# GpSimd's neighbour gathers issued by half rounds, ahead of the maxima that use them

## What is computed

```python
cand = jnp.where(mask[..., None], h[:, None, :, :], NEG)   # mask: neighbours without the node itself
mx = cand.max(axis=2)
neigh_agg = jnp.where(has_neigh, mx, h)
out = h @ W_self + b_self + neigh_agg @ W_neigh + b_neigh
...
out = relu((out - mu) * rsqrt(var + EPS) * gamma + beta)
```

## Time and profile before

| | us |
|---|---|
| median of 3 runs | 9130.13 (9124.97 to 9143.81) |
| the profiled execution | 9111.52 |
| its span, first to last instruction | 9109.8 |
| busy: TensorE, VectorE, ScalarE, GpSimd | 5148.5, 5894.4, 4402.1, 5128.1 |
| granted TensorE clock, share of full speed | 0.781 |

### The profile page before, as it was taken

The page is one execution under the profiler, slowest core; times in us unless marked ns, Lnnn a source line. Parts: engine busy times, 40 slices in busy tenths (PEclk is TensorE's granted clock), DMA queues, the critical chain, the costliest instruction groups (busy, mean ns, idle before and its releaser), DMA issues.

```text
span 9109.8 us, 178961 instructions
## 1 busy us (share of the span) xinstructions
PE 5148.5 (57%) x60584; PEld 4779.8 (52%) x60584; DVE 5894.4 (65%) x7002; ACT 4402.1 (48%) x3608; POOL 5128.1 (56%) x5234
## 2 busy tenths in 40 slices
PE   3673750365765668365865667556845667362026
PEld 3672750364755557363865567555745567361025
DVE  5874860386867788486867687687847688581024
ACT  5644730165635566165735566356715566160034
POOL 0004777377764677377764677276764677377630
PEclk9885875687877878687987888788877888686568
DMA  2114332234332533135322433234322433132210
GB/s 99 43 34 124 66 66 25 46 69 113 61 63 65 122 65 80 19 76 133 67 62 66 119 66 83 58 75 101 69 48 66 120 65 80 54 55 58 23 26 29
DMA packets 307180, 629.05 MB, mean 69 GB/s; under 512 B 113553, under 2 KB 165906, under 8 KB 270610
## 3 DMA queue, kind: packets, MB, share of 16 engines
q0 software_dynamic: 91936, 161.87, 16.9%
q1 hardware_dynamic: 212354, 456.38, 14.2%
q10 hardware_dynamic: 2160, 0.06, 0.0%
HBM read 506.89 MB, written 111.15 MB: 68 GB/s over the span
## 4 chain that ended last, share of the span: by engine, by line
POOL 20%; issue 16%; DVE 14%; PE 13%; DMA 8%; ACT 4%; POOLq 2%; DVEq 2%; ACTq 1%; SPq 0%
DMA G<-table,idx 6%; POOL G L552 6%; POOL best L552 5%; PE ps L1413 4%; POOL best L538 4%; PE ps L1386 3%; PE ps L1415 2%; POOL best L535 2%; DVE keys L1077 2%; POOL G L535 2%; ACT Pbuf L689 1%; PE ps L1438 1%; DVE key L1067 1%; POOL best L537 1%; ACT Hn L689 1%
## 5 line engine op out<-in xcount | busy, mean ns | idle before, releaser
L552 POOL DMA_INDIRECT G<-table,idx x1416 | 1502.7, 1061 | 508.5 <-issue 452.7
L1415 PE MATMUL ps<-Hn,AT 128*128 128x99 bf16 x12288 | 1774.5, 216 | 0.0
L1415 PE MATMUL ps<-X,AT 128*128 128x99 bf16 x12288 | 1735.0, 214 | 52.6 <-issue 52.6
L544 POOL DMA_DIRECT2D idx<-lists x433 | 259.3, 599 | 2445.9 <-issue 1964.9
L689 ACT ACTIVATE Hn<-Rb,q 128x2048 int8<-128x2048 f32 x768 | 1485.4, 1988 | 86.6 <-PE ps L1415 82.1
L689 ACT ACTIVATE Pbuf<-Rb,q 128x2048 int8<-128x2048 f32 x768 | 1487.8, 1987 | 18.2 <-PE ps L1415 15.6
L552 POOL DMA_INDIRECT best<-table,idx x1024 | 1093.7, 1068 | 319.4 <-issue 309.3
L1415 PEld LDWEIGHTS ps<-X,AT 128*128 128x128 fp8e4 x12288 | 1243.2, 101 | 57.6 <-issue 57.6
L1415 PEld LDWEIGHTS ps<-Hn,AT 128*128 128x128 fp8e4 x12288 | 1256.5, 102 | 0.0
L1413 PE MATMUL ps<-X,Hn 128*128 128x198 bf16 x6144 | 933.6, 268 | 567.6 <-DVE Hn L937 358.6
L1413 PE MATMUL ps<-Hn 128*128 128x198 bf16 x6144 | 960.3, 272 | 433.0 <-DVE Zs L957 236.0
(11 more groups left out here) (186 smaller groups left out, 11171.7 us busy)
## 6 DMA issues: line engine op xcount, KB each, us to landing
Rb<-in_adj SPq DMA_DIRECT2D x128, 1024.0 KB, 6.3
Rb<-rrows SPq DMA_DIRECT2D x104, 1024.0 KB, 6.3
bytes_A<-A SPq DMA_DIRECT2D x128, 256.0 KB
bytes_AT<-AT SPq DMA_DIRECT2D x128, 256.0 KB
AT<-bytes_AT SPq DMA_DIRECT2D x128, 256.0 KB, 3.6
AT<-bytes_A SPq DMA_DIRECT2D x128, 256.0 KB, 4.6
G<-table,idx POOLq DMA_INDIRECT x1416
h<-Hn SPq DMA_DIRECT2D x16, 1024.0 KB, 4.1
```

The costliest lines, as they stand in the source:

```text
L544: pool.dma_start(idx[:, slot, :], lists[bass.ds(r, 1)].rearrange("o p k -> (o p) k")).then_inc(idx_in[slot], 16)
L552: pool.indirect_dma_start(out=dst[:, k, :], out_offset=None, in_=table, in_offset=bass.IndirectOffsetOnAxis(ap=idx[:, slot, k:k + 1], axis ...
L1415: ins = pe.matmul(both[:, 0, 0:G], A8[:, jb, at], v[:, 0:G], start=False, stop=jb == T - 1, skip_group_check=True)
```

## The change

`G` becomes the accumulator, with room for 4 keys, and `best` the place where gathers land, with two halves of 4. `idx` now holds two lists, `arrived_idx`, where the next list lands, and `asked`, from which the gathers in flight read; GpSimd copies one into the other by halves (128x4 elements). `ask(r, part)` makes this copy and issues 4 gathers. In a tile but the last, the first half of the first round is copied into `G`, and its place is asked for the next round at once; the second half is folded, and asked for again; then the list two rounds on is fetched. Further rounds do the same: wait for a half, fold it, ask for the same half of the next round, which may be that of the next tile. The last round of a tile asks for the first round of the next one. The last tile of a graph doesn't ask ahead: its first round is in flight already, and it asks for each further round at its start, both halves, and fetches the next list, which at the end is that of the next graph's first round. `gather` begins with asking for the first round. The fold of `best` onto itself loses its width 4, since `G` has 4 keys. Two more lists are reserved in HBM, and in the last `middle` SyncE writes one more list behind the last round, so that the last fetch finds one.

```diff
-        G = sb("G", [P, KEYS, F])
+        G = sb("G", [P, KEYS // 2, F])
         idx = sb("idx", [P, 2, KEYS], U32)
+        asked, arrived_idx = idx[:, 0, :], idx[:, 1, :]
...
-        LN_CHAIN, LV_CHAIN, POOL_CHAIN, MERGE, TREE = 7, 12, 4, 6, 10
+        LN_CHAIN, LV_CHAIN, POOL_CHAIN, MERGE, TREE = 7, 12, 4, 8, 7
...
             def middle(b, alone):
+                if alone:
+
+                    total = sp.value_load(cum[0:1, bass.ds(B * (T + 1) - 1, 1)], min_val=0, max_val=ROUNDS)
+                    plain(sp)
+                    sp.wait_ge(idx_ready, total)
+                    sp.wait_ge(list_in, total * 16 + 16)
+                    settle(sp)
+                    sp.dma_start(lists[bass.ds(total, 1)].rearrange("o p k -> (o p) k"), found_idx[:, :]).then_inc(list_in, 16)
...
-            def fetch(r, slot):
+            def fetch(r):
 
                 plain(pool)
                 pool.wait_ge(list_in, r * 16 + 32)
-                pool.dma_start(idx[:, slot, :], lists[bass.ds(r, 1)].rearrange("o p k -> (o p) k")).then_inc(idx_in[slot], 16)
-
-            def rows_of(fetched, slot, dst):
+                pool.dma_start(arrived_idx, lists[bass.ds(r, 1)].rearrange("o p k -> (o p) k")).then_inc(idx_in, 16)
+
+            def half(part):
+                return slice(part * (KEYS // 2), (part + 1) * (KEYS // 2))
+
+            def ask(v, r, part):
 
                 plain(pool)
-                pool.wait_ge(idx_in[slot], fetched * 16)
+                pool.wait_ge(idx_in, r * 16 + 16)
                 settle(pool)
-                for k in range(KEYS):
+                v(pool.tensor_copy(asked[:, half(part)], arrived_idx[:, half(part)]))
+                settle(pool)
+                for k in range(part * (KEYS // 2), (part + 1) * (KEYS // 2)):
                     pool.indirect_dma_start(
-                        out=dst[:, k, :], out_offset=None, in_=table,
-                        in_offset=bass.IndirectOffsetOnAxis(ap=idx[:, slot, k:k + 1], axis=0)).then_inc(got[k], 16)
+                        out=best[:, k, :], out_offset=None, in_=table,
+                        in_offset=bass.IndirectOffsetOnAxis(ap=asked[:, k:k + 1], axis=0)).then_inc(got[part], 16)
+
+            def landed(r, part):
+                plain(pool)
+                pool.wait_ge(got[part], r * 64 + 64)
 
             def number(b, t):
                 return pool.value_load(cum[0:1, bass.ds(b * (T + 1) + t, 1)], min_val=0, max_val=ROUNDS)
 
             def tile(b, t, last):
                 lo, hi = number(b, t), number(b, t + 1)
-
-
-
-
-                fetch(lo if last else lo + 1, 1)
-                rows_of(b * T + t + 1, 0, best)
-                if last:
-
-                    plain(pool)
-                    pool.wait_ge(idx_in[1], lo * 16 + 16)
-                pool.sem_inc(merged, MERGE)
+                v = Chain(pool, merged, lo * MERGE, MERGE)
+                landed(lo, 0)
+                settle(pool)
+                v(pool.tensor_copy(G[:, :, :], best[:, half(0), :]))
+                if not last:
+                    ask(v, lo + 1, 0)
+                landed(lo, 1)
+                greater(v, G[:, :, :], best[:, half(1), :])
+                if not last:
+                    ask(v, lo + 1, 1)
+                    fetch(lo + 2)
+                settle(pool)
+                pool.sem_inc(merged, MERGE - v.n)
                 with pool.Fori(lo + 1, hi) as r:
+                    w = Chain(pool, merged, r * MERGE, MERGE)
                     if last:
-                        fetch(r, 1)
-                    rows_of(r + 1 if last else r, 1, G)
-                    v = Chain(pool, merged, r * MERGE, MERGE)
-                    for half in range(2):
-
-                        plain(pool)
-                        for k in range(half * KEYS // 2, (half + 1) * KEYS // 2):
-                            pool.wait_ge(got[k], r * 16 + 16)
-                        if half == 1 and not last:
-
-                            fetch(r + 1, 1)
-                        part = slice(half * KEYS // 2, (half + 1) * KEYS // 2)
-                        greater(v, best[:, part, :], G[:, part, :])
-                    v.end()
+                        for part in range(2):
+                            ask(w, r, part)
+                        fetch(r + 1)
+                    for part in range(2):
+                        landed(r, part)
+                        greater(w, G[:, :, :], best[:, half(part), :])
+                        if not last:
+                            ask(w, r + 1, part)
+                    if not last:
+                        fetch(r + 2)
+                    w.end()
                     settle(pool)
-                if not last:
-
-                    fetch(hi, 0)
                 v = Chain(pool, tree, (b * T + t) * TREE, TREE)
-                for width in (4, 2, 1):
-                    greater(v, best[:, 0:width, :], best[:, width:2 * width, :])
+                for width in (2, 1):
+                    greater(v, G[:, 0:width, :], G[:, width:2 * width, :])
                 settle(pool)
-                v(pool.tensor_copy(Agg[:, bass.ds(t, 1), :].rearrange("p o f -> p (o f)"), best[:, 0, :]))
+                v(pool.tensor_copy(Agg[:, bass.ds(t, 1), :].rearrange("p o f -> p (o f)"), G[:, 0, :]))
                 v.end()
-                if not last:
-
-                    plain(pool)
-                    pool.wait_ge(idx_in[1], hi * 16)
                 settle(pool)
 
             def gather(b):
@@ -607,7 +619,13 @@
 
                 pool.wait_ge(tab_in, b * 16 + 16)
                 settle(pool)
-                fetch(number(b, 0), 0)
+                first = number(b, 0)
+                if isinstance(b, int) and b == 0:
+                    fetch(first)
+                v = Chain(pool, first_asked, b * 2, 2)
+                for part in range(2):
+                    ask(v, first, part)
+                fetch(first + 1)
                 with pool.Fori(0, T - 1) as t:
                     tile(b, t, False)
                 tile(b, T - 1, True)
```

More of the change, by code:

```diff
@@ L190, in build @@
         bytes_AT = nc.dram_tensor("bytes_AT", [B * T, P, N], U8, kind="Internal").ap()
-        lists = nc.dram_tensor("lists", [ROUNDS + 2, P, KEYS], U32, kind="Internal").ap()
+        lists = nc.dram_tensor("lists", [ROUNDS + 4, P, KEYS], U32, kind="Internal").ap()
         h0 = nc.dram_tensor("h0", [P, T * F], F32, kind="Internal").ap()
@@ L247, in build @@
         list_in = sem("list_in")
-        idx_in = [sem("idx_in0"), sem("idx_in1")]
-        got = [sem(f"got{s}") for s in range(KEYS)]
+        idx_in = sem("idx_in")
+        got = [sem(f"got{s}") for s in range(2)]
         merged = sem("merged")
+        first_asked = sem("first_asked")
         tree = sem("tree")
```

## The result

The changed kernel takes 9220.3 us (median of 4 runs, 9213.0 to 9231.3) against 9127.6 for the kernel before: a ratio of 1.0103, 95% interval 1.0082 to 1.0125. It is slower by 93 us, 1.0%, and the prediction of 9040, in a range of 8850 to 9190, was wrong in its direction too. The profiled execution took 9222.3 us, its span is 9220.6.

The account below looks back on a forecast made before the run. GpSimd's gather stretches were taken to set the pace: 223 us added work against 320 removed waits, 97 less, 85 on the path, taken as 90 with TensorE restarting sooner. From the median of 9130.1 that gives 9040 us, range 8850 to 9190.

Parts of the forecast that it names:

- What bounds the kernel: Gather stretches, 7207 us from table to `maxima`, set the pace; GpSimd is itself busy and can gain at most its waits.
- the reading of the margins: TensorE's waits at L1343: a shorter stretch gains in seven graphs, nothing in the fifth; a longer one costs in all eight.
- The waits go: GpSimd's waits for rows and lists in the stretches, all 320 us, vanish since 10 us of work covers each landing.
- The work per tile: GpSimd's work for a tile of two rounds rises from 40.8 to 42.4 us; 223 us added work in all.
- the term of the ask: GpSimd from a fold's end through the small copy to the first gather: 1.25 us, bounds 1.0 and 1.8.
- dear first gathers: A group's first gather can be dearer, 1.37 against 0.95 us; 0.1 us for each added group, +42 us.
- The break-even: Time from fold to first gather at which the change gains nothing: 1.25 + 97 / 610 = 1.41 us.
- the rival of dear asks: Between fold and first gather an ask takes 1.8 us, 239 us net loss, all graphs pay: 9369 us; chance 0.18.
- that of no change: The terms cancel, or the lists hold GpSimd up for what was won; chance 0.10.
- the four signs of being wrong: Copy-to-gather gap over 1.0 us; mean gather over 1.10 or under 1.00; waits over 1 before folds; fetch waiting for a list.
- Landing time that doesn't depend on the load: GpSimd's waits are something else and stay, the added work comes on top: 9130 + 223 = 9353 us; chance 0.05.
- the -97: Net forecast over the gather stretches: 223 us of added work against 320 of removed waits, 97 us less, 12 per graph.

## Why the prediction was wrong, point by point

**What bounds the kernel**: right. The stretches grew by 108 us and the span by 111. What a longer stretch costs is paid, in the fifth graph too (846 to 875 us), as the reading of the margins said.

**The waits go**: right for the rows, of which 0.3 us are left. Wrong for the 33 us of waits for lists among the 320: those grew to 147.

**The work per tile**: this step failed, in the term of the ask. It stood at 1.25 us from fold to first gather. By the rows of the changed kernel it is 1.7, in four parts: about 0.22 before the small copy where the list is there, as forecast; 0.24 of waiting for a list (147.2 / 610), forecast none; 0.33 for the copy, forecast 0.2; 0.91 behind it ((1105.2 - 1830 x 0.30) / 610), forecast 0.8. That is 0.45 x 610 = 275 us over the forecast.

The folds give 67 back (all operations of `greater`, 2213 to 2146 us; why they are shorter stays open), and -97 + 275 - 67 = 111, where the stretches measured 108. That this comes so close is partly luck. The sum leaves out the gathers' own time (2596 to 2663 us, 67 where 42 was counted for dear first gathers) and the copy of 128x512 (0.74 us, not 0.6: 18 us), which bring it to 154. Of the 46 us the other way a part can be the 41.1 us (25 times) that fetches stood in the kernel before until a list was written, which the prediction counted nowhere and the changed kernel doesn't have.

The break-even had been put at 1.41 us, and this is the rival of dear asks, to which I gave 0.18. It named the place and the threshold, but not the cause: it expected the price in the two waits of the chain, and of the excess of 0.45 us these hold about 0.1. A good half, 0.24, is the wait for a list, which stood in another rival, that of no change; the rest is the longer copy.

**The fetch**: this is the wait that I missed, and the text passed over it. I priced the fetch by where it is issued (behind gathers, its preparation hidden, 0.6 us) and looked at whether the list is written, but not at when the fetch *lands*. The landing of 1.9 us belongs to a fetch issued when all gathers before it have landed; the new place is behind 4 in flight, with 3.5 to 4 us until the list is needed. There it lands after 3.7 us in the middle behind a later round, and moving it took 80 of the 108 us away. Of the four signs of being wrong that the prediction named this is the one that nearly came, as a copy that waits for a list; the gap behind the small copy (0.79), the mean gather (1.092) and the waits before folds stayed inside their limits.

**The small copy**: its median is 187 ns, near the 0.19 taken; the mean is 332. The windows view from 8404 to 8857 us, the last stretch (busy time of TensorE, its weight loads, VectorE, ScalarE and GpSimd), shows VectorE standing still; the view of line 564 (duration in ns, least, median and most) follows for that stretch, for 7000 to 7700 us, where VectorE is busy for 552 of 700 us, and for the whole run:

```profile
8404.00:8857.00 453.00, 0.00 (x0) 0.00 (x0) 0.00 (x0) 0.00 (x0) 328.12 (x412) 0.50 0.22 34
```

```profile
L564 POOL COPY idx<-idx x42: 183/183/197, 8404.3 to 8839.3; 128x4 uint32<-128x4 uint32 x42
```

```profile
L564 POOL COPY idx<-idx x58: 183/187/969, 7008.1 to 7689.2; 128x4 uint32<-128x4 uint32 x58
```

```profile
L564 POOL COPY idx<-idx x610: 181/187/4266, 750.9 to 8839.3; 128x4 uint32<-128x4 uint32 x153
```

In the stretch where VectorE stands it never takes over 197 ns, beside a busy VectorE up to 969, and 4266 in the whole run. A median hides this and a sum doesn't. The trace tells which instructions of VectorE do it (timelines of GpSimd and VectorE, one copy):

```profile
2399.63 0.90 POOL L564 COPY idx<-idx 128x4 uint32<-128x4 uint32 x1 [0.27 <-POOL G L548]
```

```profile
2398.16 2.32 DVE L945 TENSOR_TENSOR Zs<-Zs,X 128x1056 f32<-128x1056 f32 x1
```

The copy ends at 2400.53, right behind that instruction of VectorE at 2400.48. Of the 610 copies 221 begin while a TENSOR_TENSOR or SCALAR_TENSOR_TENSOR of VectorE runs, and take 590 ns on average; the 215 of them over 200 ns all end 42 to 48 ns behind the end of that instruction. The 212 that begin while VectorE stands take 185 ns on average and 203 at most, and the 117 beside its MAX8, MATCH_REPLACE8, reductions and statistics 191 at most. This is about 90 of the 203 us. The Trainium skill ("SBUF — State Buffer", section "Who interferes with whom") has it that a VectorE instruction with two SBUF inputs contends with a GpSimd instruction that reads SBUF. The trace agrees, with the numbers above.

**Landing time that doesn't depend on the load** (the last rival): fell. It said that the waits of the earlier trace rows are something else and stay; they vanished. Landings are also shorter: by the semaphore increments, a group's last gather had landed after 6.2 us on average behind 16 gathers in a row, and in the changed kernel a half's last after 4.2 us (2.9 in the middle in first rounds, 4.4 in later ones). That was also where the rule of the Trainium skill ("DMA: Bandwidth & Descriptors", section "Anatomy of one DMA — SWDGE (gpsimd) path"), 2.15 us a landing, would have led. For a list of 4 KB its rule gives an estimate of 2.0 us. The kernel before agrees in the middle (1.9 us), the changed one doesn't (3.5 us in the middle and 9.6 at most).

**The range** ended at 9190, below the forecast of the dear case (9369 at 1.8 us); the -97 rested on 610 times a price for which the prediction itself gave 1.0 to 1.8 us. Of the 336 us up to that bound the range took in 150 above the forecast, and the measured time lay 30 beyond.

## What to carry to other kernels

When an engine both issues the transfers and uses them, ask first how long it waits and how long it is busy: issuing ahead can win the first only, and each thing added per issue (a copy of 16 bytes per partition, the wait for it, a preparation that nothing covers) is paid wherever it doesn't fall into a wait: here 0.8 us of work, 0.63 us net in the old order. Price a small transfer at what it is put behind, at its landing and not its issue, and look at what the transfers in front of it read. And if indices, addresses or flags must be copied because the number of rounds isn't known, look for the rounds whose number is fixed: here that was 256 of 305, and giving them places of their own, with the copy of 128x512 and the late fetch gone as well, turned a loss of 1.0% into a gain of 2.4%.

## What was not expected of the hardware

- A 4 KB list fetched behind 4 gathers in flight lands 3.5 us after its issue in the middle, 9.6 at most; 1.9 us in the middle where the gathers have landed first. With other engines standing the 3.5 stay and the most is 3.9 us, so the long landings alone belong to other traffic.
- Gathers of 128 rows with the lists of later rounds, mostly one filler row, land after 4.4 us, those of first rounds after 2.9, and a fetch behind them after 3.7 and 2.1 us. With one first round's list in all rounds the difference is gone.
- A gather prepared behind a wait starts 0.79 us after a copy and 0.81 after a fold, as forecast; in a row of gathers the gap is 0.30. Cutting a group of 8 in two therefore costs 0.5 us without any copy, by estimate.
- A copy of 128x4 elements takes 0.18 us alone or beside VectorE's MAX8, and 0.59 on average when it begins beside a TENSOR_TENSOR or SCALAR_TENSOR_TENSOR of VectorE; over the whole run 0.33.
